# A decoder stack on one core: the tile network's last part ordered slot by slot with norm buffers of its own, and the expert layer in one unrolled block

## The chip, the cores and the metric

The kernel is written in Bass and runs on 1 core of a Trainium2 chip. The metric is the device time of the whole kernel in microseconds (us); lower is better. The engines named below are TensorE (PE, with PEld for its weight loads), VectorE (DVE), ScalarE (ACT), GpSimd (POOL) and SyncE (SP, which issues most DMAs). Each runs its own list of instructions in order, and they wait for one another on semaphores.

## The reference, cut to what matters

`x` has 32 sequences of 128 tokens with 128 numbers each, all float32. Six sublayers follow one another, each added to the stream and normalised (`x = layernorm(x + f(x))`). The change touches the third and the sixth.

```
# 3, the tile network: a learned choice of one of 64 small splines per token
scores = x @ sigs.T ; gates = calibrate(scores)      # piecewise linear between 8 knots
cluster = argmax over 8 clusters; local = argmax over the 8 tiles of that cluster
comp = tanh(gelu(x @ w1 + b1) @ w2 + b2)             # two numbers per token
mag = relu(comp @ spline_w1[tile] + spline_b1[tile]) @ spline_w2[tile] + spline_b2[tile]
y = x + mag * directions[tile] * output_scale
y = (y - mean(y)) / sqrt(var(y) + eps) * gamma + beta     # its own norm
x = layernorm(x + y)                                      # the stream's norm

# 6, the expert layer: 8 experts that share one weight, each takes 100 tokens
probs = softmax(x @ w_gate); best = argmax(probs); gate = max(probs)
place = cumulative count of best over all 4096 tokens; gate = 0 where place > 100
x = layernorm(x + gate * (x @ w_expert + b_expert))
```

## The kernel before, in words

`program` calls six functions one after the other: `min_gru`, `cross_attention`, `tile_ffn`, `self_attention`, `cross_attention`, `moe_ffn`. The stream stays on the chip as `xT`, 128 features on the partitions by 4096 tokens. A group is 4 sequences (512 tokens), so there are 8 groups; a pair is two groups (u = 0 and 1), so there are 4 pairs. Functions are separated by a barrier (`clear_counts`), and no work of one overlaps work of the next.

`tile_ffn` first computes scores (L1471), the two choices with long chains of small DVE operations (`calibrate`, `first_max_one_hot`), and between them, on PE and ACT, the compression to `comp`. DVE adds the picked scores with one strided reduction (L1633); ACT then takes their exponential (L1545), behind its own queue of gelu, tanh and a table load. The last part begins at L1650 and runs over the 4 pairs. Its steps per pair are: `one_hot` (DVE), `turn` (PE transposes, ACT copies), `rows` (PE picks each token's table row), `weigh` (7 small DVE operations), `turn_weighed` (PE, ACT), `sum` (PE matmul with the directions, DVE adds the stream: `y`), then the own norm: `square` (ACT), `variance` (PE matmul with a matrix of 1/128, ACT Ln and Exp), `gain` (DVE, two operations), and the stream's norm: `centre` (PE matmul, ACT square), `stream_variance` (PE, ACT Ln and Exp) and `divide` (DVE, writes `xT`). Most are done once for each u. One list `ORDER` sets the order for all three engines. It is made by giving every step a time within its pair (`AT`), adding 10.5 us per pair, and sorting. Both norms of a lane u use the same tiles `sq`, `logs` and `inv`, all pairs use the same `y`, and the matmuls of `sum`, `variance` and `stream_variance` write the same bank `ps_n[u]`.

`moe_ffn` has four blocks with a barrier between them: loads and masks; a loop of 4 iterations over pairs, in which ACT copies the tokens (L2148), PE computes gate logits (L2130), expert outputs (L2134) and the tokens turned back (L2138), and DVE and ACT keep the results; the routing, a chain of 18 small DVE operations with two matmuls in it; and a loop of 4 iterations for the output, in which DVE multiplies by the gate (L2255), adds the tokens (L2258), takes mean and variance with bn_stats and bn_aggr, ACT makes the inverse root of 4 columns, and DVE scales (L2274) and SP stores.

## Time and profile before

| | us |
|---|---|
| median of 3 runs (2054.84 to 2058.22) | 2057.4 |
| the profiled execution, its own time | 2057.52 |
| its span from first to last instruction | 2055.5 |
| tile network, 1043.5 to 1193.5 | 150.0 |
| of it the last part, from the first `one_hot` at 1106.5 to the last `divide` at 1193.2 | 86.7 |
| expert layer, 1976.5 to 2055.5 | 79.0 |
| mean granted clock of TensorE over the span, share of full speed | 0.901 |

Times in a timeline are microseconds from the span's start. A row gives the start, the duration, the engine and the instruction with what it writes and reads; the brackets at its end say how long the engine had been idle and which instruction ended that.
### The profile page before, as it was taken

How to read it: one execution, taken by the hardware profiler on the slowest of the kernel's cores; microseconds unless marked ns; L12 is line 12 of the kernel's file. 1: busy time of each engine (PE TensorE's matmuls, PEld its weight loads, DVE VectorE, ACT ScalarE, POOL GpSimd, SP SyncE). 2: the span in 40 equal slices, each digit the busy share in tenths (PEclk: the TensorE clock that was granted, in tenths of full speed). 3: DMA queues.
4: the chain of work that ended last, by engine and by line, in shares of the span. 5: the costliest groups of instructions: out<-in, count | busy, mean ns of one | idle time of the engine just before them, and what ended most of it. 6: DMA issues, size and time to landing. Idle time of an engine off the chain costs nothing. (4 is left out here: it accounts for less than half of the span.)

```text
span 2055.5 us, 31160 instructions
## 1 busy us (share of the span) xinstructions
PE 1695.4 (82%) x11522; PEld 986.2 (48%) x11522; DVE 1273.8 (62%) x1804; ACT 1203.0 (59%) x2497; POOL 399.5 (19%) x369
## 2 busy tenths in 40 slices
PE   3999999999999446888875748999999995888861
PEld 1444444444434125666653324666666664666651
DVE  0777777777777368777345424666666664566627
ACT  2777877777777326777821525555555553466533
POOL 0111111011011036666400001222222221110000
PEclk9999999999999656888965869999999997899985
DMA  4000000000000000000000010000000000000001
GB/s 118 1 11 1 0 11 0 0 0 0 0 1 0 8 16 4 8 2 1 2 3 0 0 42 1 1 1 1 1 1 1 1 2 13 11 8 5 2 3 41
DMA packets 36377, 16.66 MB, mean 8 GB/s; under 512 B 15286, under 2 KB 35088, under 8 KB 36240
## 3 DMA queue, kind: packets, MB, share of 16 engines
q1 hardware_dynamic: 32080, 8.91, 2.0%
q10 hardware_dynamic: 4160, 5.90, 0.8%
q8 instruction: 89, 1.46, 0.3%
q14 instruction: 48, 0.39, 0.1%
HBM read 12.71 MB, written 2.10 MB: 7 GB/s over the span
## 5 line engine op out<-in xcount | busy, mean ns | idle before, releaser
L1985 POOL TENSOR_TENSOR self_probs<-self_probs,self_rz 128x1024 f32<-128x1024 f32 x64 | 121.3, 1895 | 548.6 <-DVE self_rz L2013 548.6
L1960 ACT ACTIVATE self_probs<-self_scores,self_neg 128x128 f32<-128x128 f32 x512 | 181.4, 384 | 16.7 <-DVE self_neg L2008 16.7
L525 POOL TENSOR_SCALAR gru_decay<-gru_zgate 128x512 f32<-128x512 f32 x96 | 75.5, 787 | 591.7 <-ACT gru_zgate L478 566.4
L389 PE MATMUL gru_gate<-gru_xn,gru_whg 128*128 128x512 f32 x384 | 182.6, 598 | 3.5 <-DVE gru_xn L568 3.5
L393 PE MATMUL gru_hid<-gru_xn,gru_whg 128*128 128x512 f32 x384 | 181.4, 595 | 0.0
L401 PE MATMUL gru_out<-gru_y,gru_wo 128*128 128x512 f32 x384 | 178.1, 599 | 0.7 <-DVE gru_y L596 0.7
L1016 PE MATMUL x_turned<-const_ident,x_probs 128*77 128x128 f32 x1024 | 156.8, 302 | 11.5 <-ACT x_pt L1118 9.4
L1118 ACT ACTIVATE x_pt<-x_turned 77x512 f32<-77x512 f32 x224 | 122.3, 583 | 64.7 <-PE x_turned L1016 64.4
L1016 PEld LDWEIGHTS x_turned<-const_ident,x_probs 128*77 128x77 f32 x1024 | 128.3, 163 | 61.7 <-issue 28.5
L1210 DVE TENSOR_REDUCE x_m<-x_scores 128x16 f32<-128x1232 f32 x64 | 92.0, 1437 | 94.3 <-PE x_scores L1005 94.1
L591 DVE SCALAR_TENSOR_TENSOR gru_ghid<-gru_hid,gru_half_c,gru_sighid 128x512 f32<-128x512 f32 x96 | 71.8, 747 | 114.6 <-ACT gru_sighid L479 114.5
L596 DVE TENSOR_TENSOR_SCAN gru_y<-gru_decay,gru_value 128x516 f32<-128x516 f32 x96 | 118.3, 1232 | 3.3
L389 PEld LDWEIGHTS gru_gate<-gru_xn,gru_whg 128*128 128x128 f32 x384 | 72.7, 191 | 94.9 <-issue 94.3
L393 PEld LDWEIGHTS gru_hid<-gru_xn,gru_whg 128*128 128x128 f32 x384 | 73.5, 191 | 93.0 <-issue 93.0
L401 PEld LDWEIGHTS gru_out<-gru_y,gru_wo 128*128 128x128 f32 x384 | 70.2, 190 | 98.3 <-issue 76.0
L1960 ACT ACTIVATION_READ_ACCUMULATOR self_probs<-self_scores,self_neg 128x1 f32 x512 | 115.4, 225 | 0.0
L478 ACT ACTIVATE gru_zgate<-gru_gate,gru_bhg_c 128x512 f32<-128x512 f32 x96 | 65.9, 686 | 68.1 <-PE gru_hid L393 67.4
L344 PE MATMUL gru_stat<-gru_sq,const_ones 128*128 128x512 f32 x144 | 78.1, 633 | 28.5 <-DVE gru_sq L572 28.5
L458 ACT ACTIVATE gru_sq<-gru_h 128x512 f32<-128x512 f32 (+1 forms) x128 | 76.8, 629 | 32.5 <-DVE gru_h L601 30.1
L1946 ACT ACTIVATE self_qT<-self_bank,self_bq,self_scale 128x512 f32<-128x512 f32 x50 | 39.3, 786 | 96.4 <-PE self_bank L1882 96.4
L1030 PE MATMUL x_out<-x_pt,x_vpad 77*32 77x128 f32 x2048 | 69.4, 276 | 29.7 <-DVE x_oT L1248 17.4
L1212 DVE TENSOR_TENSOR x_dist<-x_scores,x_m 128x1232 f32<-128x1232 f32 x64 | 92.2, 1441 | 2.2
(347 smaller groups left out, 3550.3 us busy)
## 6 DMA issues: line engine op xcount, KB each, us to landing
...
```

What stands on the lines that cost most here:

```text
L344: mm(ps_stat[u][:, :], const["ones"][:, :], sq[u][:, 0, :], start=True, stop=True).then_inc(done.sem, 1)
L389: mm(ps_gate[n % 2][:, :], whg[:, l, k, DI + c * P:DI + (c + 1) * P], xn[u][:, k, :], start=(k == 0), stop=(k == KH - 1))
L393: last = mm(ps_hid[n % 2][:, :], whg[:, l, k, c * P:(c + 1) * P], xn[u][:, k, :], start=(k == 0), stop=(k == KH - 1))
L401: last = mm(ps_out[m][:, :], wo[:, l, c, m * P:(m + 1) * P], padded(y[u][:, c, :]), start=(c == 0), stop=(c == KI - 1))
L458: f(sq[u][:, m, :], hidden_chunk(u, i, m), ACT.Square).then_inc(sq_ready[u].sem, 1)
L596: v.tensor_tensor_scan(y[u][:, c, :], decay[r][:, :], value[r][:, :], 0.0, ALU.mult, ALU.add).then_inc(scan_ready.sem, 1)
L1016: last = turn_(ps_t[c % 2][0:S, j * T:(j + 1) * T], probs[n % 2][:, TILE4 * j + c, :], ident[:, :])
L1118: f(pt[n % 2][:, c, :, :].rearrange("p j t -> p (j t)"), ps_t[c % 2][0:S, :], ACT.Relu).then_inc(pt_ready[c].sem, 1)
L1210: v.tensor_reduce(top, scored(), AX.X, ALU.max).then_inc(m_ready.sem, 1)
L1212: v.tensor_tensor(dist[:, n % RING, :, :].rearrange("p (r i) s -> p r i s", i=TILE4), scored(), top.unsqueeze(3).broadcast_to([P, TILE4, T ...
L1960: last = f(probs[n % 2][:, a, jj, :], ps_s[n % 2][:, a, jj * T:(jj + 1) * T], ACT.Exp, bias=neg[n % 2][:, a, jj:jj + 1], accum_out=z[n % 2 ...
L1985: pool.tensor_tensor(probs[n % 2][:, :, :, :], probs[n % 2][:, :, :, :], whole, ALU.mult).then_inc(pn_ready.sem, 1)
```

## The change

In `tile_ffn`, `y` gets two buffers that alternate by pair, and `sq`, `logs` and `inv` exist once for the own norm and once for the stream's norm, with semaphores of their own. `ORDER` is now written slot by slot: in slot s all engines take `weigh`, `turn_weighed` and `sum` of pair s, `turn` and `rows` of pair s+1, `one_hot` of pair s+2, the own norm and `centre` of pair s-1, and the stream's norm and `divide` of pair s-2. The strided reduction over 8 clusters becomes three additions of halves. The unused class `DoubleNorm` goes.

In `moe_ffn`, the four blocks become one and the loops are unrolled. All 32 gate matmuls come first and read `xT` itself; the copies of the tokens go. The means of the expert's weight rows and of its bias are taken off once, at the start, so that the output needs no mean: the squares are summed on ACT. The bias enters the expert's bank by a matmul with 512 columns; ACT keeps the first 5 groups' expert outputs, and the last 3 stay in their banks. The routing runs on DVE while PE goes on with the groups; its two matmuls stand before the third group. The output is one multiply-add per sequence, one scaling per group, and stores from `y`, which holds all groups.

```diff
-y, sq, logs, inv = ([t.sb(f"{name}{u}", [P, GROUP]) for u in range(U)] for name in ("y", "sq", "logs", "inv"))
+y = [[t.sb(f"y{r}{u}", [P, GROUP]) for u in range(U)] for r in range(2)]
+sq, logs, inv = ([[t.sb(f"{name}{w}{u}", [P, GROUP]) for u in range(U)] for w in ("own", "str")] for name in ("sq", "logs", "inv"))
...
-ORDER = [(kind, p, u) for _, kind, p, u in sorted((p * PERIOD + at, kind, p, u) for p in range(NP) for kind, at, u in AT)]
+SLOT = (("square", -1, 0), ("stream_variance", -2, 0), ("square", -1, 1), ("stream_variance", -2, 1),
+        ("weigh", 0, 0), ("variance", -1, 0), ("turn", 1, 0), ("variance", -1, 1), ("turn", 1, 1),
+        ("divide", -2, 0), ("divide", -2, 1), ("turn_weighed", 0, 0), ("turn_weighed", 0, 1),
+        ("gain", -1, 0), ("rows", 1, 0), ("gain", -1, 1), ("rows", 1, 1), ("one_hot", 2, 0),
+        ("sum", 0, 0), ("sum", 0, 1), ("centre", -1, 0), ("centre", -1, 1))
+ORDER = [(kind, s + ahead, u) for s in range(-2, NP + 2) for kind, ahead, u in SLOT if 0 <= s + ahead < NP]
...
             elif kind == "sum":
                 pe.wait_ge(copied[u].sem, USED["turn_weighed", p, u] + 1)
                 if p:
-                    pe.wait_ge(logged[u].sem, 2 * p)
+                    pe.wait_ge(logged[0][u].sem, p)
                 mm(ps_n[u][:, :], dir_sb[:, :], ohmT[u][:, :], start=True, stop=True).then_inc(dired[u].sem, 1)
-            elif kind in ("variance", "stream_variance"):
-                n = 2 * p + (kind == "stream_variance")
-                pe.wait_ge(squared[u].sem, n + 1)
-                if kind == "stream_variance":
-                    pe.wait_ge(logged[u].sem, n)
-                mm(ps_n[u][:, :], const["mean"][:, :], sq[u][:, :], start=True, stop=True).then_inc(var_mm[u].sem, 1)
+            elif kind == "variance":
+                pe.wait_ge(squared[0][u].sem, p + 1)
+                if p:
+                    pe.wait_ge(logged[1][u].sem, p)
+                mm(ps_n[u][:, :], const["mean"][:, :], sq[0][u][:, :], start=True, stop=True).then_inc(var_mm[0][u].sem, 1)
+            elif kind == "stream_variance":
+                pe.wait_ge(squared[1][u].sem, p + 1)
+                if p + 1 < NP:
+                    pe.wait_ge(summed[u].sem, p + 2)
+                else:
+                    pe.wait_ge(logged[0][u].sem, p + 1)
+                mm(ps_n[u][:, :], const["mean"][:, :], sq[1][u][:, :], start=True, stop=True).then_inc(var_mm[1][u].sem, 1)
             elif kind == "centre":
                 pe.wait_ge(gained[u].sem, p + 1)
                 if p:
                     pe.wait_ge(divided[u].sem, p)
-                mm(ps_z[u][:, :], const["centre"][:, :], y[u][:, :], start=True, stop=True).then_inc(centred[u].sem, 1)
+                mm(ps_z[u][:, :], const["centre"][:, :], y[p % 2][u][:, :], start=True, stop=True).then_inc(centred[u].sem, 1)
...
-        def inverse(u, n):
-            act.wait_ge(var_mm[u].sem, n + 1)
-            f(logs[u][:, :], ps_n[u][:, :], ACT.Ln, bias=const["eps"][:, :]).then_inc(logged[u].sem, 1)
-            act.wait_ge(logged[u].sem, n + 1)
-            f(inv[u][:, :], logs[u][:, :], ACT.Exp, scale=-0.5).then_inc(inv_ready[u].sem, 1)
+        def inverse(w, p, u):
+            act.wait_ge(var_mm[w][u].sem, p + 1)
+            if p:
+                act.wait_ge(inv_ready[w][u].sem, p)
+            f(logs[w][u][:, :], ps_n[u][:, :], ACT.Ln, bias=const["eps"][:, :]).then_inc(logged[w][u].sem, 1)
+            act.wait_ge(logged[w][u].sem, p + 1)
+            f(inv[w][u][:, :], logs[w][u][:, :], ACT.Exp, scale=-0.5).then_inc(inv_ready[w][u].sem, 1)
...
             elif kind == "square":
                 act.wait_ge(summed[u].sem, p + 1)
                 if p:
-                    act.wait_ge(var_mm[u].sem, 2 * p)
-                f(sq[u][:, :], y[u][:, :], ACT.Square).then_inc(squared[u].sem, 1)
+                    act.wait_ge(var_mm[0][u].sem, p)
+                f(sq[0][u][:, :], y[p % 2][u][:, :], ACT.Square).then_inc(squared[0][u].sem, 1)
             elif kind == "variance":
                 if p:
-                    act.wait_ge(divided[u].sem, p)
-                inverse(u, 2 * p)
+                    act.wait_ge(gained[u].sem, p)
+                inverse(0, p, u)
             elif kind == "centre":
                 act.wait_ge(centred[u].sem, p + 1)
-                f(sq[u][:, :], ps_z[u][:, :], ACT.Square).then_inc(squared[u].sem, 1)
+                if p:
+                    act.wait_ge(var_mm[1][u].sem, p)
+                f(sq[1][u][:, :], ps_z[u][:, :], ACT.Square).then_inc(squared[1][u].sem, 1)
             elif kind == "stream_variance":
-                act.wait_ge(gained[u].sem, p + 1)
-                inverse(u, 2 * p + 1)
+                if p:
+                    act.wait_ge(divided[u].sem, p)
+                inverse(1, p, u)
...
-        v.tensor_reduce(mine[:, :, :], picked[:, :, :, :].rearrange("p b c j -> p b j c"), AX.X, ALU.add).then_inc(mine_ready.sem, 1)
+        link(v.tensor_tensor(picked[:, :, 0:4, :], picked[:, :, 0:4, :], picked[:, :, 4:8, :], ALU.add))
+        link(v.tensor_tensor(picked[:, :, 0:2, :], picked[:, :, 0:2, :], picked[:, :, 2:4, :], ALU.add))
+        v.tensor_tensor(mine[:, :, :], picked[:, :, 0, :], picked[:, :, 1, :], ALU.add).then_inc(mine_ready.sem, 1)
...
             elif kind == "sum":
                 dve.wait_ge(dired[u].sem, p + 1)
-                if p:
-                    dve.wait_ge(centred[u].sem, p)
-                v.tensor_tensor(y[u][:, :], ps_n[u][:, :], tokens(p * U + u), ALU.add).then_inc(summed[u].sem, 1)
+                if p >= 2:
+                    dve.wait_ge(centred[u].sem, p - 1)
+                v.tensor_tensor(y[p % 2][u][:, :], ps_n[u][:, :], tokens(p * U + u), ALU.add).then_inc(summed[u].sem, 1)
             elif kind == "gain":
-                dve.wait_ge(inv_ready[u].sem, 2 * p + 1)
-                link(v.scalar_tensor_tensor(y[u][:, :], y[u][:, :], gamma_c[:, 0:1], inv[u][:, :], ALU.mult, ALU.mult))
-                v.scalar_tensor_tensor(y[u][:, :], y[u][:, :], beta_c[:, 0:1], tokens(p * U + u), ALU.add, ALU.add).then_inc(gained[u].sem, 1)
+                out = y[p % 2][u][:, :]
+                dve.wait_ge(inv_ready[0][u].sem, p + 1)
+                link(v.scalar_tensor_tensor(out, out, gamma_c[:, 0:1], inv[0][u][:, :], ALU.mult, ALU.mult))
+                v.scalar_tensor_tensor(out, out, beta_c[:, 0:1], tokens(p * U + u), ALU.add, ALU.add).then_inc(gained[u].sem, 1)
             elif kind == "divide":
-                dve.wait_ge(inv_ready[u].sem, 2 * p + 2)
-                v.tensor_tensor(tokens(p * U + u), ps_z[u][:, :], inv[u][:, :], ALU.mult).then_inc(divided[u].sem, 1)
+                dve.wait_ge(inv_ready[1][u].sem, p + 1)
+                v.tensor_tensor(tokens(p * U + u), ps_z[u][:, :], inv[1][u][:, :], ALU.mult).then_inc(divided[u].sem, 1)
...
 def moe_ffn(nc, const, xT, w_gate, w_expert, b_expert, out):
 NE = B * EXPERTS
+NR = 3
+HELD = NG - NR
+be = t.sb("be", [P, GB, D])
...
+expert = t.sb("expert", [P, HELD, GROUP])
+y = t.sb("y", [P, B, D])
+sq = t.sb("sq", [P, GB, D])
+ps_l = t.ps("logits", [P, B, EXPERTS])
+ps_p = t.ps("places", [P, 2, NE])
+ps_e = [t.ps(f"expert{r}", [P, 512]) for r in range(NR)]
+ps_x = [t.ps(f"tokens{r}", [P, 512]) for r in range(NR)]
+def seq(n):
+    return xT[:, n * T:(n + 1) * T]
+def seqs(g):
+    return slice(g * GB, (g + 1) * GB)
+@block.sync
+    sp.dma_start(wg[:, :], w_gate).then_inc(wg_loaded.sem, DMA)
+    sp.dma_start(we[:, :], w_expert).then_inc(we_loaded.sem, DMA)
+    for b in range(GB):
+        sp.dma_start(be[:, b, :], b_expert.partition_broadcast(P)).then_inc(we_loaded.sem, DMA)
+    for g in range(NG):
+        sp.wait_ge(res_ready.sem, g + 1)
+        sp.dma_start(out[seqs(g)].rearrange("b t d -> t b d"), y[:, seqs(g), :]).then_inc(stored.sem, DMA)
+    sp.wait_ge(stored.sem, NG * DMA)
...
+@block.tensor
+    pe.wait_ge(wg_loaded.sem, DMA)
+    for n in range(B):
+        last = mm(ps_l[:, n, :], seq(n), wg[:, :], start=True, stop=True)
+    last.then_inc(l_mm.sem, 1)
+    pe.wait_ge(we_ready.sem, 2)
+    for g in range(NG):
+        if g == 2:
+            pe.wait_ge(shaped.sem, 2)
+            pe.wait_ge(best_ready.sem, 1)
+            flat = best[:, :, :].rearrange("p b e -> p (b e)")
+            mm(ps_p[:, 0, :], upto[:, :], flat, start=True, stop=True)
+            mm(ps_p[:, 1, :], const["ones"][:, :], flat, start=True, stop=True).then_inc(places_mm.sem, 1)
+        r = g % NR
+        if g >= NR:
+            pe.wait_ge(x_kept.sem, g - NR + 1)
+        for b in range(GB):
+            last = turn(ps_x[r][:, b * D:(b + 1) * D], seq(g * GB + b), const["ident"][:, :])
+        last.then_inc(x_mm.sem, 1)
+        if g >= NR:
+            pe.wait_ge(e_kept.sem, g - NR + 1)
+        mm(ps_e[r][:, :], const["mean"][:, :], be[:, :, :].rearrange("p b d -> p (b d)"), start=True, stop=False)
+        for b in range(GB):
+            last = mm(ps_e[r][:, b * D:(b + 1) * D], seq(g * GB + b), we[:, :], start=False, stop=(b == GB - 1))
+        last.then_inc(e_mm.sem, 1)
 @block.scalar
+    nc.scalar.preload_act_table_set(LN_EXP)
     act.wait_ge(dist_ready.sem, 1)
+    f(probs[:, :, :], probs[:, :, :], ACT.Exp).then_inc(exp_ready.sem, 1)
+    def evict(g):
+        act.wait_ge(x_mm.sem, g + 1)
+        f(xtok[:, seqs(g), :].rearrange("p b d -> p (b d)"), ps_x[g % NR][:, :], ACT.Copy).then_inc(x_kept.sem, 1)
+        if g < HELD:
+            act.wait_ge(e_mm.sem, g + 1)
+            f(expert[:, g, :], ps_e[g % NR][:, :], ACT.Copy).then_inc(e_kept.sem, 1)
+    for g in range(NG):
+        evict(g)
+    for g in range(NG):
+        act.wait_ge(y_ready.sem, g + 1)
+        for n in range(g * GB, (g + 1) * GB):
+            last = f(sq[:, n % GB, :], y[:, n, :], ACT.Square, accum_out=var[:, n:n + 1])
+        last.then_inc(var_ready.sem, 1)
+        act.wait_ge(var_ready.sem, g + 1)
+        f(logs[:, seqs(g)], var[:, seqs(g)], ACT.Ln, bias=const["eps"][:, :], scale=1.0 / D).then_inc(logged.sem, 1)
+        act.wait_ge(logged.sem, g + 1)
+        f(inv[:, seqs(g)], logs[:, seqs(g)], ACT.Exp, scale=-0.5).then_inc(inv_ready.sem, 1)
 @block.vector
+    dve.wait_ge(we_loaded.sem, (1 + GB) * DMA)
+    link(v.tensor_reduce(we_mean[:, :], we[:, :], AX.X, ALU.add))
+    link(v.tensor_reduce(be_mean[:, :], be[:, :, :], AX.X, ALU.add))
...
+    v.tensor_scalar(we[:, :], we[:, :], we_mean[:, 0:1], None, ALU.subtract).then_inc(we_ready.sem, 1)
+    v.tensor_tensor(be[:, :, :], be[:, :, :], be_mean[:, :].unsqueeze(2).broadcast_to([P, GB, D]), ALU.subtract).then_inc(we_ready.sem, 1)
+    dve.wait_ge(l_mm.sem, 1)
+    link(v.tensor_reduce(top[:, :], ps_l[:, :, :], AX.X, ALU.max))
+    v.tensor_tensor(probs[:, :, :], ps_l[:, :, :], wide(top), ALU.subtract).then_inc(dist_ready.sem, 1)
     dve.wait_ge(exp_ready.sem, 1)
...
+    link(v.tensor_tensor(best[:, :, :], probs[:, :, :], wide(gate), ALU.is_equal))
+    link(v.tensor_reduce(top[:, :], best[:, :, :], AX.X, ALU.min))
+    v.tensor_tensor(best[:, :, :], best[:, :, :], wide(top), ALU.is_equal).then_inc(best_ready.sem, 1)
     dve.wait_ge(places_mm.sem, 1)
...
+    def gated(g):
+        dve.wait_ge(x_kept.sem, g + 1)
+        if g < HELD:
+            dve.wait_ge(e_kept.sem, g + 1)
+            source = expert[:, g, :]
+        else:
+            dve.wait_ge(e_mm.sem, g + 1)
+            source = ps_e[g % NR][:, :]
+        for b in range(GB):
+            n = g * GB + b
+            last = v.scalar_tensor_tensor(y[:, n, :], source[:, b * D:(b + 1) * D], gate[:, n:n + 1], xtok[:, n, :], ALU.mult, ALU.add)
+        last.then_inc(y_ready.sem, 1)
+    def scaled(g):
+        dve.wait_ge(inv_ready.sem, g + 1)
+        v.tensor_tensor(y[:, seqs(g), :], y[:, seqs(g), :], inv[:, seqs(g)].unsqueeze(2).broadcast_to([P, GB, D]), ALU.mult).then_inc(res_ready.sem, 1)
+    for g in range(NG):
+        gated(g)
+        if g >= 2:
+            scaled(g - 2)
+    scaled(NG - 2)
+    scaled(NG - 1)
...
```

## Rows read from the trace of the kernel before

**Rows 1.** The page: busy time by engine, whole kernel.
```profile
PE 1695.4 (82%) x11522; PEld 986.2 (48%) x11522; DVE 1273.8 (62%) x1804; ACT 1203.0 (59%) x2497; POOL 399.5 (19%) x369
```

**Rows 2.** Windows, tile network's last part: PE, PEld, DVE, ACT, POOL busy, clock.
```profile
1106.50:1130.00 23.50, 19.30 (x63) 12.84 (x64) 5.11 (x11) 5.39 (x9) 0.00 (x0) 0.50 0.00 1
1146.00:1164.20 18.20, 13.75 (x49) 6.86 (x50) 8.37 (x17) 9.89 (x17) 0.00 (x0) 0.91 0.00 0
1170.00:1175.00 5.00, 2.13 (x4) 0.79 (x4) 3.48 (x9) 0.60 (x1) 0.00 (x0) 0.64 0.00 0
```

**Rows 3.** Timeline, pairs 1 and 2: start, us, engine, instruction, [idle before].
```profile
1146.02 0.69 DVE L1670 TENSOR_TENSOR ffn_y<-ffn_norm,xT 128x512 f32<-128x512 f32 x1 [9.10 <-PE ffn_norm L1512]
...
1156.73 0.59 ACT L1561 ACTIVATE ffn_ohT<-ffn_turned 64x512 f32<-64x512 f32 x1 [0.26 <-PE ffn_turned L1499]
...
1159.08 0.69 ACT L1549 ACTIVATE ffn_logs<-ffn_norm,const_eps 128x512 f32<-128x512 f32 x1 [0.32 <-PE ffn_norm L1518]
...
1159.80 0.63 ACT L1551 ACTIVATE ffn_inv<-ffn_logs 128x512 f32<-128x512 f32 x1
...
1160.38 0.63 PE L1499 MATMUL ffn_turned<-const_ident,ffn_oh 128*64 128x128 f32 x4
1160.93 0.96 PEld L1506 LDWEIGHTS ffn_rows<-ffn_table,ffn_ohT 64*128 64x128 f32 x8 [0.20 <-issue]
...
1164.18 0.69 DVE L1670 TENSOR_TENSOR ffn_y<-ffn_norm,xT 128x512 f32<-128x512 f32 x1 [8.01 <-PE ffn_norm L1512]
```

**Rows 4.** Windows: the network's scores, then the expert layer's three stages.
```profile
1048.50:1062.00 13.50, 13.50 (x64) 13.50 (x64) 3.72 (x10) 2.25 (x7) 0.00 (x0) 0.50 0.05 5
1981.40:2009.90 28.50, 22.89 (x160) 21.95 (x160) 7.05 (x16) 9.03 (x16) 0.00 (x0) 0.84 0.00 0
2009.90:2021.70 11.80, 2.08 (x4) 1.18 (x4) 7.90 (x18) 0.42 (x2) 0.00 (x0) 0.55 0.00 1
2021.70:2055.50 33.80, 0.00 (x0) 0.00 (x0) 28.40 (x120) 14.28 (x24) 0.00 (x0) 0.50 0.22 62
```

**Rows 5.** Timeline, the end of the kernel.
```profile
2050.12 2.10 DVE L2274 TENSOR_SCALAR moe_res<-moe_yt,moe_mv,moe_inv 128x128 f32<-128x128 f32 x8
2050.24 0.30 ACT L2240 ACTIVATE moe_logs<-moe_mv,const_eps 128x4 f32<-128x4 f32 x1 [0.89 <-DVE moe_mv L2267]
2050.57 0.20 ACT L2242 ACTIVATE moe_inv<-moe_logs 128x4 f32<-128x4 f32 x1
```

**Rows 6.** Timeline, the first pair of groups.
```profile
1109.18 3.67 PE L1506 MATMUL ffn_rows<-ffn_table,ffn_ohT 64*128 64x65 f32 x16
...
1114.84 0.69 DVE L1665 TENSOR_TENSOR ffn_oh<-ffn_oh,ffn_mag 128x512 f32<-128x512 f32 x1
...
1127.30 3.51 PE L1518 MATMUL ffn_norm<-ffn_sq,const_mean 128*128 128x512 f32 x4
```

**Rows 7.** Timeline, choice of clusters: a reduction, and the exponential behind it.
```profile
1081.44 3.83 DVE L1633 TENSOR_REDUCE ffn_mine<-ffn_picked 128x256 f32<-128x2048 f32 x1
...
1090.03 0.51 ACT L1545 ACTIVATE ffn_e<-ffn_mine,ffn_nit 128x256 f32<-128x256 f32 x1
```

**Rows 8.** DMA issues: KB each, median us from issue to landing.
```profile
moe_be_row<-in_L_ffn_b_expert SPq DMA_DIRECT2D x1, 64.0 KB, 3.2
...
moe_wg<-in_L_ffn_w_gate SPq DMA_DIRECT2D x1, 4.0 KB, 2.0
```

**Rows 9.** Timeline, expert matmuls of two groups.
```profile
1983.74 1.83 PEld L2134 LDWEIGHTS moe_bank_e<-moe_we,moe_xs 128*128 128x128 f32 x8
...
1990.51 0.97 PEld L2130 LDWEIGHTS moe_bank_g<-moe_wg,moe_xs 128*128 128x128 f32 x8 [1.55 <-ACT moe_xs L2148]
```

**Rows 10.** Timeline, self attention: activations with a summed output.
```profile
1250.68 0.36 ACT L1960 ACTIVATE self_probs<-self_scores,self_neg 128x128 f32<-128x128 f32 x1
1250.93 0.20 ACT L1960 ACTIVATION_READ_ACCUMULATOR self_probs<-self_scores,self_neg 128x1 f32 x1
1251.02 0.36 ACT L1960 ACTIVATE self_probs<-self_scores,self_neg 128x128 f32<-128x128 f32 x1
```

218 lines of the change are left out of this document (35 added, 183 removed).

## The prediction

> **What bounds the kernel now.** I read the page first, then windows, then the timeline of the two changed stretches. The page calls PE the busiest engine with 82% [rows 1], but that is an average over six functions, four of which the change leaves alone. In the tile network's last part no engine is full: in the third period PE is busy 13.75 of 18.20 us, ACT 9.89, DVE 8.37 [rows 2]. What sets the period is a chain. DVE idles 9.10 us before the `sum` of pair 1 and 8.01 us before that of pair 2, both until PE delivers, and the two stand 18.16 us apart [rows 3]. Within one period the list runs a lane's own norm and its stream norm one behind the other, on one `sq`, `logs` and `inv`. The granted clock is at its lower level, 1.2 GHz, for the first 23.5 us, and drops again where PE has gaps (0.64 in a window in which PE is busy 2.13 of 5 us) [rows 2].
>
> In the expert layer the three stages are read from their windows [rows 4]: in the groups' matmuls (28.5 us) PE is busy 22.89; the routing (11.8) is a chain on DVE with PE all but idle; in the output (33.8) DVE is busy 28.40, so DVE bounds it. They follow one another and no stage hides another.
>
> **The tile network's last part, step by step.** Prices at the higher level, 2.4 GHz: turn of a lane 0.5 (the row of four shows 0.63 with its latency), `rows` of a lane 0.97, Ln with Exp 1.35, copy 0.6 [rows 3]. A 512-column matmul is 3.51/2 = 1.75 at 1.2 GHz [rows 6], so about 0.88 at 2.4, and 1.1 where its result is awaited; squares are taken as 0.63 like the Exp.
>
> Slots -2 to 0: the first `rows` end at 1112.9 (1109.18 + 3.67) and the first `weigh` at 1115.5 [rows 6], as now. Then PE, at 1.2 GHz, turns the weighed pair until 1117.5, does `rows` of pair 1 (3.6) and two sums (3.5): 1124.6. Slot 1: two variances and two turns of pair 2 take 5.4, to 1130; if the clock then rises as it does now, one turn waits for ACT's copy until 1131.1, and 0.5 + 1.94 + 1.76 (sums) + 1.76 (centres) lead to 1137.1.
>
> Slot 2 is the full slot. From the end of the previous centre, ACT's queue is: second centre square 0.7, square 0.65, stream inverse 1.35, square 0.6, stream inverse 1.35, own inverse 1.35, copy 0.6, own inverse 1.35, copy 0.6, together 8.55. Only then may PE turn the second weighed lane (0.6), and behind it come `rows` 1.94, sums 1.76 and centres 1.76, with a wait of 0.1: 14.8 in all. DVE has 8.9 of work in it, ACT 10.7, PE 10.9; the new waits (Ln after the previous Exp, a square after the previous variance of its norm) were met a slot earlier and cost nothing, and the shared bank `ps_n` is used three times a slot for 1.1 + 0.7 each, 5.4 of 14.8; the chain decides, not an engine. Slot 3 has no turn or `rows` of a new pair: ACT 7.35 + copy 0.6, then 3.5 on PE: 11.5. The rest, slots 4 and 5, is 7.35, gain 1.6, centre 1.1, square 0.7, variance 1.1, inverse 1.35, divide 0.7 with waits: 14.6. Ends: 1137.1, 1151.9, 1163.4, 1178.0, against 1193.2: 15.2 less. What PE's gaps of over 2 us in slots 3 to 5 cost in clock lies between nothing and four matmuls of 0.88 more (3.5); I take the middle, 1.7. So 13.5 less. Bounds: if slot 1 stays at 1.2 GHz, 5.4 more, so 8; if the clock rises with the first sums, 3.5 us less from both slots together, so 17.
>
> **The fold of the reduction.** It takes 3.83 us now [rows 7]; three additions of 1024, 512 and 256 columns cost about 2.4 (0.69 per 512 as in the `sum` row of [rows 3]). But ACT's exponential starts only at 1090.03, 4.8 us after the reduction ends [rows 7], behind its gelu, tanh and table load. The gain is nothing; without that cover it would be 1.4.
>
> **The expert layer, step by step.** SP issues 6 loads in place of 3 ahead of everything. The gate weights land 2.0 us after their issue [rows 8], so PE starts at 1978.6, while its stage starts at 1981.4 now [rows 4]. The bias now comes four times, the last issued at about 1979.3 and landed 3.2 later [rows 8]; DVE needs some 2.5 us to centre it: 1985. That is hidden behind the gate matmuls, 8 us long or more; uncovered it would cost what it is late.
>
> Gate matmuls: 32, each two weight loads. In the scores stretch 64 weight loads with 72-column matmuls took 13.50 us with the clock at 0.50 all through [rows 4], so this stream, with 8 columns, will stay there too: 14.1, ending 1992.8. Groups: turns 0.87, bias 1.75, experts 1.83 [rows 9] make 4.4 at 1.2 GHz; 0.5 + 0.88 + 0.97 = 2.35 at 2.4. I take one group at the lower and seven at the higher level, since the 512-column matmul makes them denser than those of now, which reach 0.84 on average [rows 4]; places matmuls 0.9. PE ends at 2014.5 and the last turned tokens come at 2012.7. The whole routing of 11.8 us, begun at 1992.8, would end near 2006 even with the 1.7 us that its matmuls wait for the third group: hidden. The new wait on PE, before the third group, has six groups queued behind it, and ACT's evictions and squares behind those; it ends at about 1998, five of DVE's us after the gate matmuls, and PE comes to it at 1999.5. Were the routing later, each us would move the end by one.
>
> ACT's evictions all stand before its squares, so the output starts at 2013.4. Per group ACT does four summed squares at a pitch of 0.34 [rows 10] and Ln with Exp, 0.53 and their hand-over [rows 5]: 1.95. DVE has four multiply-adds at 0.26, the pitch of the scalings (2.10 for 8) [rows 5], and one scaling of 0.69: 1.75, just below ACT; at 0.34 each it would be 2.05 and add 1 us. Eight groups: 2029.0; the last scaling 0.75 and the tail of now (2055.5 - 2052.2 = 3.3): 2033.1. I keep 0.9 for hand-overs: 2034.0, or 21.5 less. Bounds: PE at 1.2 GHz throughout 7.8 less; squares at 0.27 (their shorter input path: no pointer bias) and an earlier rise 24.
>
> A rule for the price of the squares: the Trainium skill, "ScalarE: Activation LUTs", section "What ACT_TABLE_LOAD costs", gives an ACTIVATE with immediate operands 186 ns + 0.833 ns per column and an overlap of about 93 ns back to back. Four squares would be 0.8 by it, and the sum about 2.5 us lower, where DVE would take over; it says nothing of the read of the sum, which this trace shows at 0.20 each.
>
> **Sum.** 13.5 + 0 + 21.5 = 35.0. The profiled execution took 2057.52 and the runs have a median of 2057.4; the difference is nothing here. 2057.4 - 35.0 = 2022.4.
>
> **Rivals.** A change within 0.2% (4.1 us) counts as the same.
> *The groups stay at 1.2 GHz.* Each then takes 4.4, the last turned tokens come 13.7 later: 2036.1. For it: the lower level held through the whole scores stretch. Against it: groups with fewer columns reach 0.84 now. Chance 0.12. The Trainium skill, "TensorE: Matmul & The Clock Gate", section "Part 4: PE-mode transpose", says that transposes do not count towards the higher clock, and a fifth of each group is transposes; that would end here.
> *ACT's squares do not overlap their reads.* 0.36 + 0.20 [rows 10] makes 2.24 for four instead of 1.37, times 8: +7.0, so 2029.4. Against it: the rows overlap. Chance 0.12.
> *The slots do not do what they say.* Engines still take steps in one fixed order, and if PE is at 1.2 GHz, a full slot is 21.8 of pure PE work instead of 14.8; slots 1 and 3 to 5 grow by some 14. The last part then is 5.8 slower than now: 2041.7. Chance 0.08.
> *Both clock cases at once*: 2041.7 + 13.7 = 2055.4, the same. Chance 0.03.
> *Slower.* Later functions start 13.5 us earlier against whatever decides the clock, and between the two changed parts, 1193.5 to 1976.5 by the table, PE is the busiest engine, as it is overall [rows 1]. It decides from the point where 39 us of that work fall from 2.4 to 1.2 GHz, since each costs as much again; then 2022.4 + 39 = 2061.4. Their code is unchanged and the runs of before lie within 3.4 us: chance 0.03.
>
> **How the numbers follow.** My forecast has 0.62, its own range 2016 to 2029 from the bounds above. 0.62 + 0.12 + 0.12 + 0.08 + 0.03 + 0.03 = 1. The range 2015 to 2038 leaves out the last three cases (0.14) and a little at the low end. Faster 0.94, same 0.03, slower 0.03.
>
> **What would show it.** Right: two `sum` rows of one lane 14 to 15.5 us apart in the full slot; `divide` of pair 3 ends about 72 us after the first `one_hot`; the second exponential no earlier relative to the scores; 64 gate weight loads in about 14 us at 0.50; groups 2.4 us apart at 1.00; ACT without gaps in the output, 1.95 per group, and 57 to 58 us for the expert layer. Wrong: a granted clock near 0.5 in the slots or groups, DVE as the bound of the output, or self attention of another length.

## The result, and the profile after

The changed kernel takes 2019.6 us (median of 4 runs, 2018.86 to 2021.67) against 2057.4 before (2054.84 to 2058.22): a ratio of 0.982 with a 95% interval of 0.9803 to 0.9837, 37.8 us less. The forecast was 2022.4, in a range of 2015 to 2038.

The page, busy time by engine of the whole changed kernel, beside [rows 1]:

```profile
PE 1695.7 (84%) x11538; PEld 988.3 (49%) x11538; DVE 1252.9 (62%) x1715; ACT 1200.1 (59%) x2551; POOL 400.2 (20%) x369
```

PE does the same work as before to 0.3 us. DVE gives up 20.9 us: 19.5 in the expert layer (43.3 in its windows of [rows 4], 23.8 in those below) and 1.5 in the fold of the reduction. So the kernel did not get shorter by less work on its busiest engine: the span went from 2055.5 to 2018.3 because work of different engines now lies over each other in two places. The two profiles split the 37.2 us like this: the tile network's last part, from its first one-hot product to the end of the last `divide`, took 86.7 and takes 74.4 (12.3 less); the expert layer, counted from the last write of `xT` ahead of it to the end of the span, took 79.7 and takes 54.1 (25.6 less); the 782.6 between them are now 783.2.

**The tile network's last part.** Windows of the changed kernel: one up to 1130, where the forecast lets the clock rise within slot 1, one for the rest of slot 1, one each for slots 2 and 3, and slots 4 and 5 in one; columns as in [rows 2] (busy time of PE, PEld, DVE, ACT, POOL, granted clock, DMA share, GB/s):

```profile
1106.60:1130.00 23.40, 21.52 (x76) 14.48 (x76) 9.65 (x21) 7.56 (x13) 0.00 (x0) 0.53 0.00 1
1130.00:1138.90 8.90, 7.91 (x29) 4.41 (x30) 5.82 (x12) 2.51 (x5) 0.00 (x0) 0.81 0.00 0
1138.90:1156.20 17.30, 15.05 (x49) 7.03 (x49) 8.11 (x15) 9.10 (x17) 0.00 (x0) 0.80 0.01 1
1156.20:1167.20 11.00, 8.72 (x25) 3.29 (x24) 5.59 (x8) 8.00 (x14) 0.00 (x0) 1.00 0.00 0
1167.20:1181.00 13.80, 8.06 (x16) 2.28 (x16) 5.65 (x8) 10.18 (x17) 0.00 (x0) 1.00 0.00 0
```

The slots were forecast to end at 1137.1, 1151.9, 1163.4 and 1178.0; they end at 1138.9, 1156.2, 1167.2 and 1181.0. Slot 3 is 0.5 shorter than forecast, slots 4 and 5 together 0.8 shorter; slots 1 and 2 are longer by 1.8 and 2.5. The clock column says why: 0.80 and 0.81 where 1.00 was assumed. Timeline of PE in slot 2 of the changed kernel:

```profile
1144.87 0.60 PE L1466 MATMUL ffn_turned<-const_ident,ffn_oh 128*64 128x128 f32 x4 [0.85 <-ACT ffn_ohT L1536]
1146.59 0.60 PE L1466 MATMUL ffn_turned<-const_ident,ffn_oh 128*64 128x128 f32 x4 [1.12 <-ACT ffn_ohT L1536]
1147.12 2.00 PE L1473 MATMUL ffn_rows<-ffn_table,ffn_ohT 64*128 64x65 f32 x16
1148.95 3.63 PE L1479 MATMUL ffn_norm<-ffn_ohmT,ffn_dirs 64*128 64x512 f32 x4
1152.51 3.63 PE L1496 MATMUL ffn_centred<-ffn_y,const_centre 128*128 128x512 f32 x4
1155.98 1.98 PE L1491 MATMUL ffn_norm<-ffn_sqstr,const_mean 128*128 128x512 f32 x4
```

The chain is the one forecast: PE stands still until ACT has copied the second turned lane, then works without a gap. But the sums and centres took 3.63 for four, 1.2 GHz, where the variances behind them took 1.98 for four, 2.4 GHz. The level fell inside a stretch in which PE was busy without pause, after two gaps of 0.85 and 1.12 us.

**The expert layer.** Windows of the changed kernel over the gate matmuls, the groups and the output, beside [rows 4]:

```profile
1967.50:1981.40 13.90, 13.86 (x65) 13.86 (x66) 2.39 (x7) 0.00 (x0) 0.00 (x0) 0.50 0.08 18
1981.40:2000.50 19.10, 19.10 (x108) 14.78 (x108) 10.76 (x29) 7.48 (x14) 0.00 (x0) 0.90 0.00 1
2000.50:2015.20 14.70, 1.27 (x9) 0.86 (x7) 10.69 (x28) 13.51 (x81) 0.00 (x0) 0.68 0.39 122
```

Three stages of 28.5, 11.8 and 33.8 us became 13.9 + 19.1 and 14.7: the routing has no stage of its own any more, PE is busy 19.10 of 19.10 us over it. In the output ACT is busy 13.51 of 14.70, and DVE, which had 28.40 of 33.8, has 10.69. Timeline of the changed kernel where the output begins, and one group of it:

```profile
2000.05 0.60 ACT L2151 ACTIVATE moe_xtok<-moe_tokens 128x512 f32<-128x512 f32 x1 [1.59 <-PE moe_tokens L2132]
2000.55 0.30 ACT L2161 ACTIVATE moe_sq<-moe_y 128x128 f32<-128x128 f32 x1
2000.75 0.19 ACT L2161 ACTIVATION_READ_ACCUMULATOR moe_sq<-moe_y 128x1 f32 x1
2000.84 0.30 ACT L2161 ACTIVATE moe_sq<-moe_y 128x128 f32<-128x128 f32 x1
...
2002.41 0.69 DVE L2223 TENSOR_TENSOR moe_y<-moe_y,moe_inv 128x512 f32<-128x512 f32 x1 [6.90 <-ACT moe_inv L2166]
...
2005.88 0.69 DVE L2223 TENSOR_TENSOR moe_y<-moe_y,moe_inv 128x512 f32<-128x512 f32 x1
...
2006.49 1.12 DVE L2218 SCALAR_TENSOR_TENSOR moe_y<-moe_expert,moe_gate,moe_xtok 128x128 f32<-128x128 f32 x4
...
2007.61 0.69 DVE L2223 TENSOR_TENSOR moe_y<-moe_y,moe_inv 128x512 f32<-128x512 f32 x1
...
2012.82 0.69 DVE L2223 TENSOR_TENSOR moe_y<-moe_y,moe_inv 128x512 f32<-128x512 f32 x1 [1.04 <-ACT moe_inv L2166]
2014.55 0.69 DVE L2223 TENSOR_TENSOR moe_y<-moe_y,moe_inv 128x512 f32<-128x512 f32 x1 [1.04 <-ACT moe_inv L2166]
```

Squares start every 0.29 us, reads of their sums at 0.19 lying over them. A group takes 1.73 us (2007.61 - 2005.88). DVE is idle for 6.90 us before its first scaling. In the middle groups it shows no idle time: 0.61 + 1.12 fill the 1.73. At the end, where it has no multiply-adds left, its last two scalings still come 1.73 apart, each after 1.04 us in which it waited for ACT. So ACT sets the pitch at the end; whether DVE sets it as well in the middle, the timeline alone doesn't tell.

### The profile page after: what moved, and what is told of

It is laid out like the page before. It is cut to its first block and busy times, and to the rows that moved or that the text cites. A ratio compares the mean times of both kernels' runs of the same rounds, so it can differ in the third digit from the quotient of the medians.

```text
span 2018.3 us, 30939 instructions
## 1 busy us (share of the span) xinstructions
PE 1695.7 (84%) x11538; PEld 988.3 (49%) x11538; DVE 1252.9 (62%) x1715; ACT 1200.1 (59%) x2551; POOL 400.2 (20%) x369
## 6 DMA issues: line engine op xcount, KB each, us to landing
gru_wo<-in_L_attn_Wo ACTq DMA_DIRECT2D x4, 384.0 KB, 10.9
```

## The experiments

Two lengths are used below. The *tile part* is counted from the first turned one-hot lane behind PE's 19.16 us of idleness to the end of the last `divide`; by that count it took 85.8 before (1107.37 to 1193.20) and 73.6 after (1107.45 to 1181.04). The *layer* is counted from the first gate matmul to the end of the span: 50.8 after (1967.54 to 2018.3). In six profiles in which this layer's code is that of the changed kernel it took 50.8 to 51.5. The kernel before had medians of 2054.5 to 2057.4 us in four series of runs, and the changed kernel was in the first of them only. So a total time that lies one to three us from the changed kernel's is not told apart from it; the small effects are read from the lengths of the part and the layer, in one profile each.

### One part alone, twice

The first kernel is the one before with only the new tile network:

> The kernel before with only the tile network's last part replaced. Theory (the two parts add up, and the work between them is untouched): its first one-hot matmul to its last divide takes 74.4 us as in the changed kernel, where the kernel before took 86.7, so the run is 12.3 us shorter, near 2045.1 us, a ratio of 0.994. Rival (the gain of one part leans on the other, through the granted clock that later stretches get): the total differs from that by more than 3 us, in the stretch between the last divide and the expert layer's first transfer, which was 782.6 us before and 783.2 after.

The second is the one before with only the new expert layer:

> The kernel before with only the expert layer replaced. Theory (the parts add up): the layer takes 54.1 us from its first transfer's issue to the end of the span, where it took 79.7, so the run is 25.6 us shorter, near 2031.8 us, a ratio of 0.988; the clock comes up at the first group's end as in the changed kernel. Rival: after the old tile network the clock history differs, and the layer's groups stay at 1.2 GHz, which by the first group's 4.3 us against 2.2 would cost 6 x 2.1 = 13 us, for 2045 us.

Measured on one chip: 2044.56 (ratio 0.9947, 0.9914 to 0.9979) and 2030.22 (0.9889, 0.9872 to 0.9905). Tile part in the first: 1104.65 to 1178.25, 73.6, and from there to the end 862.6, as before (862.3). In the second the tile part takes 86.3 and the layer 51.3. Savings of 0.5% and 1.1% make 1.6% where both parts together save 1.8%, within the intervals: the parts add up, neither rival holds, and the layer's clock does not lean on the tile network.

### Order or buffers

Two kernels divide the tile part's edit. One keeps the new buffers and brings back the old order; the waits are changed to fit it.

```diff
-        SLOT = (("square", -1, 0), ("stream_variance", -2, 0), ...
-        ORDER = [(kind, s + ahead, u) for s in range(-2, NP + 2) for kind, ahead, u in SLOT if 0 <= s + ahead < NP]
+        PERIOD = 10.5
+        AT = (("one_hot", 0, 0), ("turn", 1, 0), ("turn", 1.5, 1), ("rows", 3, 0), ...
+        ORDER = [(kind, p, u) for _, kind, p, u in sorted((p * PERIOD + at, kind, p, u) for p in range(NP) for kind, at, u in AT)]
```

> The changed kernel with its norm buffers of their own for each unit, but the parts of the tile network issued in the order of the kernel before (two periods over two pairs of units, each lane's parts after the other's). Theory of the prediction (the order brings the gain, since it puts the other unit's matmuls into each unit's chain of norm steps): the part is back near 86.7 us, the run 12 us longer than the changed kernel, near 2031.8 us. Rival (the buffers bring it, by letting the norms of two units overlap): the part stays near 74.4 us and the run near 2019.6.

The other keeps the slots, and the two norms share `sq`, `logs` and `inv` again (`y` keeps its two buffers). For that the stream's variance comes ahead of the own norm's square in each slot, and the waits follow:

```diff
-        sq, logs, inv = ([[t.sb(f"{name}{w}{u}", [P, GROUP]) for u in range(U)] for w in ("own", "str")] for name in ("sq", "logs", "inv"))
+        sq, logs, inv = ([[t.sb(f"{name}{u}", [P, GROUP]) for u in range(U)]] * 2 for name in ("sq", "logs", "inv"))
-        SLOT = (("square", -1, 0), ("stream_variance", -2, 0), ("square", -1, 1), ("stream_variance", -2, 1),
+        SLOT = (("stream_variance", -2, 0), ("square", -1, 0), ("stream_variance", -2, 1), ("square", -1, 1),
```

> The changed kernel with its slot order, but one set of buffers for squares, logarithms and inverses for each lane, as in the kernel before, so a unit's squares wait until the unit two slots earlier has used its inverse. Theory of the prediction (order alone carries the gain; what the shared buffers cost is that the variance's stream comes ahead of the squares in a slot): 0.4 to 0.5 us more for each full slot, 1 to 1.5 us in all, near 2021 us. Rival (the buffers carry the gain): the part is back near 86.7 us and the run near 2032.

The old order with new buffers: 2027.54 (0.9868, 0.9852 to 0.9885), tile part 86.3 (1101.92 to 1188.19). The gains of the pairs 1 and 2 stand as far apart as in the kernel with the old tile network, 18.29:

```profile
1144.84 0.75 DVE L1651 SCALAR_TENSOR_TENSOR ffn_y<-ffn_y,ffn_gamma,ffn_invown 128x512 f32<-128x512 f32 x1 [1.52 <-ACT ffn_invown L1522]
...
1163.13 0.75 DVE L1651 SCALAR_TENSOR_TENSOR ffn_y<-ffn_y,ffn_gamma,ffn_invown 128x512 f32<-128x512 f32 x1 [1.52 <-ACT ffn_invown L1522]
```

So buffers of their own are worth nothing under the old order. The slots with shared buffers: 2020.45 (0.9829, 0.9805 to 0.9854), 7.1 us less than the old order in the same series, tile part 80.5. That is 5.8 less than the old order and 6.9 more than the changed kernel's profile, where 1 to 1.5 was expected. But most of the 6.9 is clock. Windows over the tile part: before, changed kernel, shared buffers, and another profile of the slots with own buffers (the last kernel below):

```profile
1107.37:1193.20 85.83, 64.06 (x192) 32.12 (x192) 33.13 (x63) 39.32 (x64) 0.00 (x0) 0.77 0.00 0
1107.45:1181.04 73.59, 61.27 (x192) 31.45 (x192) 34.02 (x63) 37.35 (x64) 0.00 (x0) 0.79 0.00 1
1102.88:1183.36 80.48, 67.10 (x192) 34.33 (x192) 34.10 (x63) 37.90 (x64) 0.00 (x0) 0.73 0.00 1
1104.54:1182.77 78.23, 66.69 (x192) 33.86 (x192) 34.02 (x63) 37.43 (x64) 0.00 (x0) 0.72 0.00 1
```

The same 192 matmul records keep PE busy for 61.27 to 67.10 us, by the clock. What is left of each length, the time in which PE stands still, is 21.8 before, 12.3 after, 13.4 with shared buffers and 11.5 in the last. By that count sharing costs 1.1 to 1.9 us, about what was expected, and by the medians of the runs 0.8. ACT's timeline with shared buffers, slot 2:

```profile
1134.86 0.60 ACT L1549 ACTIVATE ffn_sq<-ffn_centred 128x512 f32<-128x512 f32 x1 [6.91 <-PE ffn_centred L1496]
1136.31 0.60 ACT L1549 ACTIVATE ffn_sq<-ffn_centred 128x512 f32<-128x512 f32 x1 [0.85 <-PE ffn_centred L1496]
1137.49 0.69 ACT L1524 ACTIVATE ffn_logs<-ffn_norm,const_eps 128x512 f32<-128x512 f32 x1 [0.59 <-PE ffn_norm L1491]
...
1138.74 0.61 ACT L1541 ACTIVATE ffn_sq<-ffn_y 128x512 f32<-128x512 f32 x1
```

The square that filled the wait for the variance in the changed kernel must now follow the logarithm and exponential, and ACT stands 0.59 us in front of them (0.89 in the next slot); PE in turn waits 1.33 for that square. The order carries nearly all of the gain; the norm buffers are worth one to two us, and only once the order uses them. The second buffer of `y` was not tested under the new order.

### What the clock does to the slots

> The changed kernel with one more matmul of 512 columns, whose result nothing reads, issued in each full slot of the tile network ahead of the transpose of the weighed rows, where TensorE stood idle for 1.08 and 1.36 us. Theory (the short gaps are what the clock falls after: it fell to 1.2 GHz some us behind each of them, and slots 1 and 2 took 8.9 and 17.3 us where 7.7 and 14.8 were forecast): with the gap filled the granted clock of the two slots is near 1.00, and some 3 to 4 us go, near 2016 us. Rival (the clock falls for another reason): the clock stays at 0.80 there and the time at 2019.6 us or a little above.

```diff
+                        if kind == "turn_weighed" and p:
+                            ...
+                            mm(ps_z[u][:, :], const["mean"][:, :], scores[:, :, :].rearrange("p b n -> p (b n)")[:, 0:512], start=True, stop=True)
```

Measured 2021.61 (0.9838, 0.9804 to 0.9872), the tile part 73.6 as without the fillers. The waits of 0.85 and 1.12 us ahead of the two turns were gone and 0.26. Windows of this kernel over 9.5 us from the middle of slot 1, and over the sums and centres of slot 2:

```profile
1129.60:1139.10 9.50, 9.44 (x40) 4.94 (x38) 6.05 (x13) 4.56 (x9) 0.00 (x0) 1.00 0.00 1
...
1148.60:1156.40 7.80, 7.74 (x11) 2.55 (x11) 3.69 (x9) 2.91 (x5) 0.00 (x0) 0.63 0.00 0
```

Slot 1 ran at 1.00 there and ended 2.1 us earlier than in the changed kernel, which looks like a success. But slot 2 fell all the same, with its gap filled, and slots 3 to 5 took 27.2 us at a mean of 0.87 where they had taken 24.8 at 1.00. The kernel of the squares below, whose tile network is that of the changed kernel with no filler, did the same (the same two stretches):

```profile
1127.20:1136.70 9.50, 8.50 (x33) 4.39 (x34) 5.99 (x13) 4.75 (x10) 0.00 (x0) 1.00 0.00 1
...
1146.20:1154.00 7.80, 7.74 (x12) 2.56 (x10) 3.33 (x10) 3.11 (x6) 0.00 (x0) 0.63 0.00 0
```

So these gaps are not what makes slots 1 and 2 fall, and my theory of them is refuted. The longest wait of PE, 2.28 us in slot 4, no experiment filled. The centres behind it, in the kernel of the squares and in the changed kernel:

```profile
1169.59 3.40 PE L1496 MATMUL ffn_centred<-ffn_y,const_centre 128*128 128x512 f32 x4 [2.28 <-DVE ffn_y L1656]
```

```profile
1174.20 1.12 PE L1496 MATMUL ffn_centred<-ffn_y,const_centre 128*128 128x512 f32 x2 [2.28 <-DVE ffn_y L1656]
```

In the changed kernel and in the kernel with the new tile network alone the level stayed up behind it, 6.8 us from there to the last `divide`; in the six other profiles of the slots with own buffers, that of the fillers among them, it was down for part of that stretch, which took 7.7 to 8.9. So a fall behind this wait is usual and not certain, and costs 0.8 to 2.1 us; that the wait causes it is not shown.

With this part's code that of the changed kernel, the tile part took 73.6 (after), 73.6, 72.1, 75.4, 77.0, 77.0 and 78.2 us in seven profiles; in three with the old order 85.8, 86.3 and 86.3. PE was busy for 60.1 to 66.7 us of it in the seven, so nearly all of that spread is clock; it stood still for 11.5 to 12.3 us, and for 21.6 to 21.8 in the three with the old order. What makes the level fall within dense work, and why at other moments in each execution, stays open. The gain of the part is therefore 8 to 14 us in a pair of profiles, 10.9 by the medians (86.3 - 75.4), and not always the 12.2 of the first pair; the time that PE no longer stands still is 9.3 to 10.3 of it, whatever the clock does.

### The reduction

```diff
-                link(v.tensor_tensor(picked[:, :, 0:4, :], picked[:, :, 0:4, :], picked[:, :, 4:8, :], ALU.add))
-                link(v.tensor_tensor(picked[:, :, 0:2, :], picked[:, :, 0:2, :], picked[:, :, 2:4, :], ALU.add))
-                v.tensor_tensor(mine[:, :, :], picked[:, :, 0, :], picked[:, :, 1, :], ALU.add).then_inc(mine_ready.sem, 1)
+                v.tensor_reduce(mine[:, :, :], picked[:, :, :, :].rearrange("p b c j -> p b j c"), AX.X, ALU.add).then_inc(mine_ready.sem, 1)
```

> The changed kernel with the sum over the rows before it formed by the one strided reduction of the kernel before, and not by the fold of additions. Theory of the prediction (the reduction lies under other work): the exponential that follows it starts within 0.2 us of where it does in the changed kernel, and the time is the same, 2019.6 us. Rival (uncovered): 1.4 us more.

Measured 2018.71 (0.9817, 0.9794 to 0.9839), 0.9 below the changed kernel's median. Timeline with the old reduction:

```profile
1080.18 3.83 DVE L1612 TENSOR_REDUCE ffn_mine<-ffn_picked 128x256 f32<-128x2048 f32 x1
...
1088.77 0.51 ACT L1518 ACTIVATE ffn_e<-ffn_mine,ffn_nit 128x256 f32<-128x256 f32 x1
```

The reduction ends 4.8 us before the exponential (1088.77 - 1084.01), as in [rows 7]; in the changed kernel the fold ends 9.1 before it. Either way the exponential starts 1.8 us after ACT's own activation for `comp` (L1515, at 1086.98 here and 1088.33 in the changed kernel), which waits for PE. Counted from the first scores matmul it even comes 2.9 us earlier than in the changed kernel, by PE's clock, so the expected agreement within 0.2 us was missed, but the rival wants it later, not earlier.

### The layer: what the clock waits for

> The changed kernel with the expert layer's gate matmuls no longer all ahead of the groups: each group's gate matmuls (8 of 64) are followed by that group's transposes of the tokens, which ScalarE evicts first. The amount of work is the same. The 64 gate matmuls took 13.8 us at 1.2 GHz in the changed kernel, and the clock came up 3.9 us into the transposes. Theory A (the transposes bring the clock up, and once up it stays through the short gate matmuls): only the first group or two run at 1.2 GHz, and the rest of the gate matmuls take half, some 5 to 6 us less in all, near 2014 us. Theory B (the clock comes up only in a stretch without the gate matmuls): nothing gained, or some us lost where the groups lose the clock too, 2019.6 to 2026 us.

```diff
+                for g in range(NG):
+                    for n in range(g * GB, (g + 1) * GB):
+                        last = mm(ps_l[:, n, :], seq(n), wg[:, :], start=True, stop=True)
+                    ...
+                    for b in range(GB):
+                        last = turn(ps_x[g % NR][:, b * D:(b + 1) * D], seq(g * GB + b), const["ident"][:, :])
```

Measured 2018.23 (0.9807, 0.9784 to 0.9831), layer 51.2, as unchanged: theory B. PE's timeline of this kernel, last pair of gates and turns, then the first groups:

```profile
1984.99 1.71 PE L2119 MATMUL moe_logits<-moe_wg,xT 128*128 128x8 f32 x8
1986.55 1.09 PE L2125 MATMUL moe_tokens<-const_ident,xT 128*128 128x128 f32 x4
1987.44 1.91 PE L2139 MATMUL moe_expert<-moe_be,const_mean 128*128 128x512 f32 x2
...
1990.85 1.89 PE L2139 MATMUL moe_expert<-moe_be,const_mean 128*128 128x512 f32 x2
1992.56 1.07 PE L2141 MATMUL moe_expert<-moe_we,xT 128*128 128x128 f32 x8
```

The 19.8 us of gates with turns, PE never idle, passed at 0.50; eight turns of four took 1.09 each to the last. The level rose some 5 us behind the first matmul of the bias, as it did 3.3 us behind it in the changed kernel. That row bears on the rule that I had made a rival of (the Trainium skill, "TensorE: Matmul & The Clock Gate", section "Part 4: PE-mode transpose": transposes do not count towards the higher clock): it agrees, though gates alone did no better, so the row does not single out the transposes. Where the rival went wrong is in what it drew from the rule: a fifth of transposes in each group did not keep the groups down.

The next kernel puts part of the gates behind two groups:

```diff
-                for n in range(B):
+                for n in range(5 * B // 8):
                     ...
                 for g in range(NG):
                     if g == 2:
+                        for n in range(5 * B // 8, B):
+                            last = mm(ps_l[:, n, :], seq(n), wg[:, :], start=True, stop=True)
+                        last.then_inc(l_mm.sem, 1)
+                    if g == 5:
```

> The changed kernel with the expert layer's gate matmuls in two parts: those of 20 of the 32 sequences ahead of the groups, and those of the other 12 behind the second group, where the clock was already at 2.4 GHz; the places come ahead of the sixth group, ScalarE's exponential ahead of the third group's eviction. The work is the same. Theory A (the clock comes up with the groups' matmuls of the bias, and once up it stays through the short gate matmuls): the 24 of 64 records of gate matmuls take 2.6 us where they took 5.2 at 1.2 GHz, TensorE ends the layer 2.6 us earlier, and the time is 2017.0 us. Theory B (the short gate matmuls bring the clock down, as their loads leave the array little to do): they start fast and the group behind them takes 4.3 us where it took 2.2, so 0 gained or 1 to 2 us lost, 2019.6 to 2021.6 us.

Measured 2017.15 (0.9796, 0.9762 to 0.9831), layer 49.7, 1.1 less than after and 1.1 to 1.8 below the six unchanged layers, where 2.6 was expected. PE's timeline:

```profile
1966.21 8.70 PE L2118 MATMUL moe_logits<-moe_wg,xT 128*128 128x8 f32 x40 [5.25 <-DMA moe_wg<-in_L_ffn_w_gate]
1975.30 1.11 PE L2135 MATMUL moe_tokens<-const_ident,xT 128*128 128x128 f32 x4 [0.39 <-DVE moe_be L2185]
...
1980.48 1.35 PE L2140 MATMUL moe_expert<-moe_be,const_mean 128*128 128x512 f32 x2
...
1982.56 2.74 PE L2123 MATMUL moe_logits<-moe_wg,xT 128*128 128x8 f32 x24
1985.16 0.64 PE L2135 MATMUL moe_tokens<-const_ident,xT 128*128 128x128 f32 x4
```

24 records of the same matmuls took 2.74 us here and 5.2 (24 x 8.70/40) ahead of the groups, and the group behind them stayed fast. Once up, the level survives 2.7 us of short matmuls; what it doesn't do is rise in them. Of the 2.5 us that the 24 records saved, 0.39 went into PE's wait for the centred bias, no longer hidden, and 0.9 into the first two groups, which took 7.3 where they had taken 6.4, since the level rose later in them: the mechanism of theory A with under half its size.

### The layer: what sets the output

This kernel leaves out the squares of two of the four sequences in each group:

> The changed kernel, but in the expert layer's output the squares of only two of the four sequences of each group are taken, so the variance of every other sequence is left out (a constant stands in for it). This takes 2 x 0.29 us of ACT from each group of four. Theory A (ACT alone sets the pitch of 1.735 us in the output): eight groups at 0.58 less, 4.6 us less, 2015.0 us. Theory B (DVE's 0.61 + 1.13 = 1.74 us in a group sets it as well): less than 0.3 us, 2019.4 us.

```diff
-                    for n in range(g * GB, (g + 1) * GB):
+                    for n in range(g * GB, (g + 1) * GB, 2):
                         last = f(sq[:, n % GB, :], y[:, n, :], ACT.Square, accum_out=var[:, n:n + 1])
```

Measured 2015.11 (0.9791, 0.9762 to 0.982), layer 48.2, 2.6 less than after: between the theories. DVE's timeline of this kernel:

```profile
2001.20 0.69 DVE L2225 TENSOR_TENSOR moe_y<-moe_y,moe_inv 128x512 f32<-128x512 f32 x1
...
2002.84 0.68 DVE L2225 TENSOR_TENSOR moe_y<-moe_y,moe_inv 128x512 f32<-128x512 f32 x1
...
2006.11 2.10 DVE L2225 TENSOR_TENSOR moe_y<-moe_y,moe_inv 128x512 f32<-128x512 f32 x3
```

Freed from ACT, DVE runs at 1.64 a group, not 1.74: in the changed kernel it had been waiting 0.1 us a group behind rows that look full. Its single multiply-adds are no shorter for it (0.345 us each here, 0.344 in the changed kernel), so it was a wait and not slower work. ACT alone sets the pitch there, and DVE is 0.1 behind it. And DVE has less left than eight full groups, since three groups' multiply-adds are done before the output starts: 8 x 0.61 + 5 x 1.03 = 10.0 against ACT's 8 x 1.73 = 13.8. The three scalings in a row at the end are that backlog; their stores leave together, and the tail takes 3.5 us where it took 3.1.

That, and the 6.90 us of idle DVE, led to the last kernel, which only moves ACT's norm steps:

```diff
                 for g in range(NG):
                     evict(g)
-                for g in range(NG):
+                    if g >= 4:
+                        norm(g - 4)
+                for g in range(NG - 4, NG):
+                    norm(g)
```

> The changed kernel with ScalarE's norm steps (four squares, logarithm, exponential) of the first four groups placed between its evictions of the groups four to seven, and no longer all behind the last eviction. The work is the same. In the changed kernel ScalarE stood idle 1.54 and 1.59 us ahead of its last two evictions, and VectorE 6.90 us ahead of its first scaling. Theory A (the output starts late only because ScalarE's queue has every norm behind the last eviction, which TensorE sets): from the fifth group's eviction ScalarE has no idle time left, 3.1 us go, and the time is 2016.5 us. Theory B (VectorE's 1.74 us of work in a group is what sets the output, or TensorE waits for the evictions that now come later): less than 0.5 us, 2019.4 us.

Measured 2017.06 (0.9798, 0.9764 to 0.9832), layer 47.7: 3.0 less than after, theory A. Windows of this kernel, from the fifth group's last eviction to the last exponential, and 7.5 us out of it:

```profile
1997.05:2012.95 15.90, 6.53 (x42) 4.90 (x40) 10.33 (x29) 15.39 (x84) 0.00 (x0) 0.84 0.32 101
1998.00:2005.50 7.50, 5.58 (x37) 4.28 (x35) 5.15 (x15) 7.28 (x40) 0.00 (x0) 1.00 0.24 74
```

ACT is busy 15.39 of the 15.90 us, and 7.28 of 7.50 while PE still computes. The run time is 2.6 below the changed kernel's median, but the intervals of the two overlap, as they do for the split gates and the halved squares; it is the layer's length, one profile of each, that shows the 3.0. Its own tile part was the longest of the seven, 78.2.

## Why the prediction held, point by point

The time came 2.8 us below the forecast, inside its own range. The parts missed in opposite directions: 12.3 where 13.5 was said, 25.6 where 21.5 was said, and 0.6 back between them. That the total is as near as it is owes something to luck: by the medians of the profiles the tile part is worth 10.9, not 12.3.

*The chain in the tile network.* Right, and shown: the order brings the gain, the buffers alone nothing. Slots 3 to 5 came within 0.8 us. The term that was mis-sized is the clock: 1.7 us were allowed, for gaps in the slots 3 to 5. These ran at 1.00 in this profile, and the loss came in slots 1 and 2, 4.3 us. Of the signs named, two missed by it: the `sum` rows of a lane in the full slot are 16.5 and 17.3 us apart (1134.46 to 1150.91, 1135.32 to 1152.62) where 14 to 15.5 was said, and the last `divide` ends 74.4 us after the first one-hot product where 72 was said. The allowance itself was about right for the place it was meant for: six of eight profiles lose 0.8 to 2.1 us behind the long wait of slot 4. What the sum lacked is the loss in slots 1 and 2, which came with the short gaps filled as well. (The terms written out for slot 2 add up to 14.7, not 14.8.)

*The fold.* Right at nothing.

*Gate matmuls and groups.* 13.8 at 0.50 (14.1 said), a first group of 4.2 (4.4), seven of 2.19 (2.35). The window of 0.50 in [rows 4] was the right neighbour for the gates, and "one group at the lower level" was right too. The rival in which the groups stay at 1.2 GHz is refuted by every profile of the new layer.

*Bias loads and the routing.* The DMA rows of the changed kernel:

```profile
moe_be<-in_L_ffn_b_expert SPq DMA_DIRECT2D x4, 64.0 KB, 5.6
moe_we<-in_L_ffn_w_expert SPq DMA_DIRECT2D x1, 64.0 KB, 2.3
```

5.6 us at the median of the four, where 3.2 was taken from the single load of [rows 8]. DVE ended the centring at 1976.3, 11.4 us after the first load's issue (1964.93) where 8.5 was said, but still 5 us before PE came; the split gates showed the price once that cover is gone, 0.39. The routing ended at 1992.2, 8.3 us before the output.

*The output.* The start was 1.3 us earlier than said (35.6 after the issue of the layer's first load, 36.9 said), the eight groups 1.73 each and not 1.95. This is the term that was most off: squares at 0.29 were priced by the 0.34 of [rows 10], which is 8 x 4 x 0.05 = 1.6 us, and the 0.9 kept for hand-overs did not appear. With the start and a tail of 3.1 for 3.3 that is 4.0 of the 4.1 by which the layer beat its forecast. The activations of [rows 10] are exponentials of attention scores with a bias by pointer; which of these differences makes the 0.05, no run separates. The 0.27 named for a square at the low end was nearer. The rule of the Trainium skill ("ScalarE: Activation LUTs", section "What ACT_TABLE_LOAD costs") makes four squares 0.8 us; the rows show 1.17 (4 x 0.29), and between every two squares they show the read of the sum, 0.19 each, of which the section says nothing. The measurement decides. (With four squares at 0.8 and DVE at 1.75 a group, the prediction's sum would fall by 8 x 0.20 = 1.6 us; it reaches the 2.5 named there only if the 0.9 for hand-overs goes too.)

*The slower rival.* The stretch between the parts took 781.2 to 783.2 us in every profile, 782.6 before: nothing like the 39 us that this rival needs.
